# Shorter expert choice on VectorE, the bias added in eight pieces, rows of maxima moved behind a weighing, and the multiply by the reciprocal sums on GpSimd

## The reference

```python
def layer(x):                                    # x: (16, 128, 32, 32) f32
    xs = reshape(ln_c(x), (16, 1024, 128))       # LayerNorm over channels, then 1024 tokens
    q, k, v = 8 heads of 16 each                 # xs @ Wq, Wk, Wv
    att = softmax(q @ k.T / sqrt(16))            # per image and head: 1024 x 1024
    out = (att @ v) @ Wproj + bproj
    x1  = x + reshape(out)
    t   = to_tokens(x1)                          # (16, 1024, 128)
    raw_gates = softmax(ln_t(t) @ w_gating)      # 16 experts
    gate_1, index_1 = max(raw_gates), argmax(raw_gates)
    mask_1 = one_hot(index_1)
    gate_2, index_2 = max, argmax of raw_gates * (1 - mask_1)
    mask_2 = one_hot(index_2)
    gate_1, gate_2 = each / (gate_1 + gate_2 + 1e-9)
    # position of each token in its expert's queue: running counts of mask_1 and mask_2, cut at 256
    # experts: relu(rows @ w1[e]) @ w2[e], weighted by gate_1 and gate_2 and summed per token
    return from_tokens(t + experts(ln_t(t)))
```

## Time and profile before

| what | value |
|---|---|
| three runs | 2253.78, 2254.86, 2256.43 us |
| the profiled execution's own time | 2254.34 us |
| its span in the trace | 2252.5 us |
| TensorE busy | 2106.4 us, 94% |
| VectorE busy | 1841.2 us, 82% |
| ScalarE busy | 1528.6 us, 68% |
| GpSimd busy | 1048.7 us, 47% |
| weight loads on TensorE | 1175.1 us, 52% |

### The profile page before, as it was taken

One profiled execution on the slowest core, in us unless ns is written; L12 is line 12 of the kernel. 1 busy time (PEld: TensorE's weight loads), 2 busy tenths in 40 slices (PEclk: granted clock), 3 DMA queues, 4 the chain that ended last, 5 costly groups with the idle time before them and its releaser, 6 DMA issues. The chain is left out here.

```text
span 2252.5 us, 53329 instructions
## 1 busy us (share of the span) xinstructions
PE 2106.4 (94%) x16914; PEld 1175.1 (52%) x16914; DVE 1841.2 (82%) x4370; ACT 1528.6 (68%) x3169; POOL 1048.7 (47%) x1650
## 2 busy tenths in 40 slices
PE   5999999999999999999999999999969999899996
PEld 2333333334333333334333333333339999899996
DVE  6899999999999999999999999999925445345664
ACT  1777777777777777777777777777646566466552
POOL 3204454454445455454445455444246577455542
PEclk7999999999999999999999999999989999999997
DMA  5223323132323323232323323223162223222586
GB/s 127 48 44 63 60 58 76 36 71 45 69 53 72 61 53 74 37 70 51 67 52 68 71 43 74 39 60 57 40 190 70 71 71 86 78 71 71 159 253 178
DMA packets 135695, 171.09 MB, mean 76 GB/s; under 512 B 31568, under 2 KB 101592, under 8 KB 135414
## 3 DMA queue, kind: packets, MB, share of 16 engines
q1 hardware_dynamic: 118582, 134.25, 27.9%
q0 software_dynamic: 16896, 34.12, 4.3%
HBM read 64.86 MB, written 48.87 MB: 50 GB/s over the span
## 5 line engine op out<-in xcount | busy, mean ns | idle before, releaser
L1009 DVE TENSOR_REDUCE sb_m_red<-banks 128x1 f32<-128x512 f32 x2048 | 1318.8, 678 | 85.6 <-PE banks L1531 79.7
L848 ACT ACTIVATE sb_arena_a<-banks 128x512 f32<-128x512 f32 x2048 | 1088.7, 600 | 329.4 <-PE banks L1555 325.7
L1555 PE MATMUL banks<-sb_arena_b 64*128 64x512 f32 x2048 | 788.7, 460 | 21.5 <-DVE sb_res L1068 9.6
L1531 PE MATMUL banks<-sb_arena_b 62*128 62x512 f32 x2048 | 741.9, 448 | 40.4 <-DVE sb_m_red L1009 27.4
L1531 PEld LDWEIGHTS banks<-sb_arena_b 62*128 62x128 f32 x2048 | 340.7, 188 | 571.7 <-DVE sb_m_red L1009 468.5
L1572 PE MATMUL banks<-sb_arena_a,sb_arena_d 128*32 128x512 f32 x4096 | 546.0, 605 | 11.0 <-DVE sb_o_t L1041 9.3
L777 POOL DMA_INDIRECT sorted_rows<-sb_rows,sb_place x256 | 250.8, 980 | 343.3 <-PE banks L1555 325.4
L1555 PEld LDWEIGHTS banks<-sb_arena_b 64*128 64x128 f32 x2048 | 331.6, 185 | 139.5 <-ACT sb_arena_a L848 95.5
L821 POOL DMA_INDIRECT expert_out<-sb_arena_d x272 | 271.6, 999 | 242.6 <-DVE sb_arena_d L1401 178.1
L1685 PE MATMUL banks<-sb_arena_d,sb_arena_c 128*128 128x128 f32 x2176 | 290.4, 277 | 1.2 <-ACT sb_arena_d L954 0.7
L1694 PE MATMUL banks<-sb_arena_c 128*128 128x128 f32 x2176 | 289.0, 276 | 0.0
(11 more groups left out here) (167 smaller groups left out, 1597.4 us busy)
## 6 DMA issues: line engine op xcount, KB each, us to landing
sb_arena_b<-sb_arena_c SPq DMA_DIRECT2D x768, 64.0 KB, 2.3
sb_arena_d<-sorted_rows SPq DMA_DIRECT2D x272, 66.0 KB
sb_x_in<-in_x_dram SPq DMA_DIRECT2D x16, 512.0 KB, 3.9
sb_res<-in_x_dram SPq DMA_DIRECT2D x16, 512.0 KB, 3.6
...
expert_out<-sb_arena_d POOLq DMA_INDIRECT x272
sorted_rows<-sb_rows,sb_place POOLq DMA_INDIRECT x256
...
```

Source lines behind the costliest of these rows:

```text
L848: nc.scalar.activation(probs[:, u % PRING, :], front("score", b, u), ACT.Exp, scale=SCALE).then_inc(exp_done, 1)
L1009: nc.vector.tensor_reduce(out=m_red[:, s % 2, at:at + 1], in_=ps_max[:, m % MRING, :], axis=AX.X, op=ALU.max).then_inc(max_taken, 1)
L1531: nc.tensor.matmul(ps_max[:, m % MRING, :], qs[rows_of, g, l, half * HALF + t * P:half * HALF + (t + 1) * P], ks[rows_of, g, l, kh * HALF: ...
L1555: nc.tensor.matmul(to, ks[rows_of, g, l, i * P:(i + 1) * P], qs[rows_of, g, l, half * HALF:(half + 1) * HALF], start=True, stop=True).then ...
```

## The change

1. **Expert choice.** The first choice is made on the shifted logits (their maximum is zero), the gates are never normalised before the choice, and ties are resolved by `scalar_tensor_tensor` with two operations in one instruction. VectorE keeps 12 instructions in a stream of its own: `top_logit` at unit 46, `choose_experts` from unit 54 (ten steps), `reciprocal_of_gates` at unit 76. GpSimd takes over scaling and shifting the logits (L708, L713 in the new kernel), one multiply of the second choice (`rank_second`, L718), and eight small instructions that finish the masks and the sum of the two gates (`finish_masks`, L724 to L744).
2. **Division.** `divide` on VectorE keeps transpose and reciprocal (units 4, 5); the multiply by the reciprocal sums is `scale_o` on GpSimd, in its queue; the transpose for the projection moves from unit 7 to 10. `divide` of the next stage waits for it (`o_scaled`).
3. **Bias** in eight instructions of 128 x 128 instead of one of 128 x 1024.
4. **Places on TensorE.** x transposes from units 1 and 5 to 3 and 11, counts from 77 to 78, rows of maxima from slot 24 to slot 26 of each stage. Slot 26 stands right behind a weighing.

The core of the diff (the tables and the new functions; where the new steps are called; the removed steps of `choose_experts` are cut):

```diff
-MSLOT = 24
+MSLOT = 26
-NORMS = 14
+NORMS = 10
...
-XT_AT, QK_AT, V_AT = (1, 5), (33, 41, 44, 48), (62, 66)
-OUT_AT, TOK_AT, LOGITS_AT, COUNT_AT, ROWS_AT = (14, 18), (20, 22), 36, 77, (74, 82)
-GATE_AT, CHOOSE_AT = 38, 44
+XT_AT, QK_AT, V_AT = (3, 11), (33, 41, 44, 48), (62, 66)
+OUT_AT, TOK_AT, LOGITS_AT, COUNT_AT, ROWS_AT = (14, 18), (20, 22), 36, 78, (74, 82)
+TOP_AT, FIRST_AT, GATE_EXP_AT, RECIP_AT = 46, 54, 50, 76
+DIVIDE_AT = (4, 5, 10)
...
+            def scale_o(b, s):
+
+                g, half = s // 2, s % 2
+                wait_apart(gp, gp_passed, norm_steps, norms_before(b, s) + 2)
+                nc.gpsimd.tensor_tensor(out=o_n[:, half, :, D * g:D * (g + 1)], in0=o_t[:, :, 0:D],
+                                        in1=o_rec[:, :].unsqueeze(2).to_broadcast([P, HALF // 32, D]),
+                                        op=ALU.mult).then_inc(o_scaled, 1)
+
             def add_bias(b):
                 wait_apart(gp, gp_passed, res_loaded, 16 * (b + 1))
-                r3 = res[:, :].rearrange("p (j c) -> p j c", j=TB)
-                nc.gpsimd.tensor_tensor(out=r3, in0=r3, in1=bias[:, :].unsqueeze(1).to_broadcast([P, TB, C]),
-                                        op=ALU.add).then_inc(res_ready, 1)
+                for j in range(TB):
+                    nc.gpsimd.tensor_tensor(out=res[:, j * C:(j + 1) * C], in0=res[:, j * C:(j + 1) * C], in1=bias[:, :],
+                                            op=ALU.add).then_inc(res_ready, 1)
...
                 place_v(b, 1)
+                if not first:
+                    scale_o(b - 1, 3)
...
+                for i in range(4):
+                    if not last:
+                        split_qk(b + 1, i)
+                    if not first and i < 2:
+                        (scale_logits, shift_logits)[i](b - 1)
+                    if i == 0:
+                        scale_o(b, 0)
+                if not first:
+                    rank_second(b - 1)
+                    finish_masks(b - 1)
                 if not last:
-                    for i in range(4):
-                        split_qk(b + 1, i)
                     place_v(b + 1, 0)
+                scale_o(b, 1)
                 add_bias(b)
+                if first:
+                    scale_o(b, 2)
                 if not first:
                     for _ in place_rows(b - 1):
                         pass
                     if b == EARLY:
                         keep_counts()
                     for n in range(16 if last else 8):
+                        if n == 2:
+                            scale_o(b, 2)
                         scatter(b - 1, n, at + 96 + (2 if last else 4) * n)
...
+            scale_o(B - 1, 3)
...
-                    if 4 <= u % UNITS < 8 and not (first and u < UNITS):
-                        divide(b, u // UNITS - 1, u % UNITS - 4)
+                    if u % UNITS in DIVIDE_AT and not (first and u < UNITS):
+                        divide(b, u // UNITS - 1, DIVIDE_AT.index(u % UNITS))
...
-                        if u == GATE_AT:
-                            gate = choose(b - 1)
-                        if GATE_AT <= u < GATE_AT + 3:
-                            next(gate)
-                        if u == CHOOSE_AT:
+                        if u == TOP_AT:
+                            top_logit(b - 1)
+                        if u == FIRST_AT:
                             choice = choose_experts(b - 1)
-                        if u >= CHOOSE_AT and u % UNITS not in BUSY:
+                        if FIRST_AT <= u < FIRST_AT + 20 and u % UNITS not in BUSY:
                             next(choice, None)
+                        if u == RECIP_AT:
+                            reciprocal_of_gates(b - 1)
```

More of the change, by code:

```diff
@@ L1040, in divide @@
                     wait(dve, pv_done, 8 * (k + 1))
+                    wait(dve, o_scaled, k)
                     nc.vector.transpose(o_t[:, :, :].rearrange("p n d -> p (n d)"), ps_pv[:, :]).then_inc(norm_steps, 1)
@@ L1112, in choose_experts @@
+                step(nc.vector.tensor_tensor(out=m1, in0=tmp2[:, :, :], in1=wide(small[:, 5, :]), op=ALU.is_equal))
+                yield
                 wait(dve, gate_exp, b + 1)
@@ L1371, in _ @@
             batch(B - 1, False, True)
-            for step in range(4):
+            for step in range(3):
                 divide(B, -1, step)
```

182 lines of the change are left out of this document (95 added, 87 removed).

## The result

The changed kernel takes 2238.59 us (median of four, 2237.93 to 2240.41) against 2254.94 of the kernel before: a ratio of 0.9925, with an interval of 0.9913 to 0.9937. That is 16.4 us less, where 31.9 less were forecast. The direction was right and the time lies in the range, but near its upper end: half of the gain did not come.

A forecast was written before the change was run, and what follows sets the result against it. TensorE and ScalarE were taken to set the pace, with VectorE felt in a few groups. Terms of 1.85 us per image gave 25.9 for images 1 to 14, plus 0.5 and 5.1: 31.5 less, 2223 us, range 2208 to 2240.

The forecast's parts named there:

- What bounds the kernel: Free pace set by TensorE and ScalarE, 2.64 us a group; VectorE felt at three or four places, about 2.5 of 100.8.
- the rival of VectorE as the bound: Every microsecond removed from VectorE would count, 5.3 us per image, giving 2171 us; chance 0.04.
- Expert choice, 0.70 at 51 to 55: Units 51 to 55: a load waited 1.19 for a maximum; moving choice steps off VectorE gains 0.70 us per image.
- 0.49 at 107 to 111: Units 107 to 111, 0.49 us over the free pace: loss taken as gone, since no choice step stands there now.
- Counts, 0.20: Units 75 to 79: 0.51 of waiting for VectorE goes, 0.3 given back at unit 78; gain 0.20 us per image.
- x transposes, 0.59: Unit 1's group gains 0.59 us per image; unit 3 costs what 5 did, unit 11 hides in unit 17's residual wait.
- Multiply, 0.17: Multiply moved to GpSimd: VectorE reaches the residual ahead of unit 17 earlier, gaining 0.17 us per image.
- Rows of maxima, +0.10 - 0.40: Slot 24 to 26, per image: transposes behind the weighing gain 0.10 us, rows late at units 0 and 96 lose 0.40.
- Image 15, 5.1: Image 15 gains 5.1 us once: 2.59 from the stop, 1.11 from the half clock, 1.4 from blocked groups.
- Image 0, 0.5: Image 0, which has no choice, gains 0.5 us.
- The rival of rows that land late (2261): Rows at stage starts take 3.65 us from issue to score everywhere, not 2.68; slower, 2261 us; chance 0.08.
- The rival of GpSimd giving nothing back: Multiply waits in GpSimd's queue or VectorE stands locked out, some 5 us per image; 2252 us; chance 0.06.

## Why the prediction was right and where it failed

The forecast had 1.85 us per image, measured were 0.87. Term by term, with what the runs showed:

- **What bounds the kernel** was right: the free pace is TensorE's and ScalarE's, and VectorE is felt only in a few groups. 18 more instructions of 7.0 us per image cost 0.8, so the rival of VectorE as the bound (2171) falls.
- **Expert choice, 0.70 at 51 to 55**: right, 0.70, and by the cause named: 2.64 in image 0 of the kernel before, which has no choice, and 3.14 again with work put back at 44 to 49.
- **0.49 at 107 to 111**: right in size and wrong in its cause. The text gave it to the choice, with "none at 107" as what is new. There was none at 107 before either: that a step stood behind nearly every maximum "until its end", as the part on the change has it, holds only to unit 77. The last step of the choice in image 8 of the kernel before (VectorE's timeline) ran some 21 us ahead of that group:

```profile
925.41 0.19 DVE L1172 RECIPROCAL sb_small<-sb_small 128x8 f32<-128x8 f32 x1
```

It was the division, by the kernel with the old division, by the kernel before with the transpose at 10, and by the 3.14 of image 0. The size came out right by luck, because the same change moved both.
- **Counts, 0.20**: nothing. The step that failed is "of which I take 0.51 as lost": a load that waits 0.56 for VectorE was followed by one that waited for ScalarE, and that second wait ended at the same time with or without the first, 1.29 after the group's start. The 0.3 given back for the place at 78 was nothing too.
- **x transposes, 0.59**: 0.25 by the groups of units 1 and 3, 0.31 by the run that puts them back (beside rows at slot 26). The gain of 0.54 to 0.59 at unit 1 and the hidden cost at unit 11 were right; "should cost what that did", of unit 3 against unit 5, was not, by 0.29.
- **Multiply, 0.17**: too small. 0.19 shows at units 11 to 15, but off VectorE it is worth 0.60 per image (100.47 with it on VectorE, against 99.87): 0.34 before the residual and 0.24 at 111 to 115, where the transpose alone would have put a new block. The whole division is worth 0.8 to 0.9 per image, more than the choice, and the prediction had 0.17 for it and the 0.49 in the wrong place. GpSimd's longer queue cost nothing in images 0 to 14: 621 ns each, and no wait for it appears. In image 15 the last two transposes for the projection wait 2.3 and 8.0 us for it; the stretch after the last score is 0.4 us longer in all, and whether that is the reason was not tried.
- **Rows of maxima, +0.10 - 0.40**: -0.78 measured. The lateness was predicted well: 0.62 at units 0 and 96 against 0.63, and from issue to score 2.66 (855.21 - 852.55, below) against 2.68. What was wrong is what follows from it. The lateness costs nothing: the group that ends at unit 3 takes 2.64 with it, and so does the one that ends at 99 once the stack DMAs go ahead. But the two DMAs, two units later, hold three stack DMAs in SyncE's queue for which TensorE waits at unit 99 (0.54). The prediction counted the moved step's own DMAs and not what is queued behind them. Behind a weighing the rows cost 3.17 and not less than 3.13.

```profile
852.55 1.36 SPq L423 DMA_DIRECT2D sb_arena_b<-sb_m_row  x2
...
855.21 0.19 PEld L1591 LDWEIGHTS banks<-sb_arena_b 64*128 64x128 f32 x2 [0.44 <-DMA sb_arena_b<-sb_m_row]
```

- **Image 15, 5.1**: 5.0, in part by luck. The stop and the half clock gave 2.57 and 1.11, as forecast (2.59 and 1.11), though in the changed kernel the moved choice alone ends the stop and the pieces add nothing. The other 1.4 was put down to "the groups that are blocked as in other images", and these were not blocked in image 15 (units 51 to 55 took 2.65 and 107 to 111 took 2.60 before). In their place came 0.64 by which the image's first score starts later, 0.49 at 11 to 15, 0.54 at 31 to 35 and 0.27 at 67 to 71, less 0.38 at 39 to 43.
- **Image 0, 0.5**: -1.0. Unit 99 costs 0.54, the score of unit 128 comes 0.64 later (which image 1 gives back), and the rows and unit 32 cost 0.4; units 107 to 111 give 0.49, and x at unit 11 costs nothing in the end (0.56 at 11 to 15, 0.55 given back by unit 23). Unit 1 gives 0.74, but units 3 to 8 take 0.62 more: they lie where the clock is still low after the start (it rises at 65.8 us before and at 66.9 after), and with other kernels they took 4.24 to 5.87. So this part says little of the change.
- **The rival of rows that land late (2261)** did not come: 2.66 at units 0 and 96. It had named the right step and the wrong mechanism. **The rival of GpSimd giving nothing back** falls with 8.3 us lost when the multiply returns to VectorE, though VectorE's own two-input instructions are still stretched beside GpSimd (0.74 against 0.28).

The misses by groups are 0.48 for the rows, 0.34 for x (0.05 at unit 1, 0.29 at unit 3), 0.20 for the counts, and -0.04 at units 11 to 19 (0.21 against 0.17): 0.98, which is 1.85 - 0.87. The prediction as a whole was right in sign and range and twice too large, half of that for one queue, and two of its terms (0.49 per image, and 1.4 of image 15) have the right size for a wrong reason.

## What to carry to other kernels

A wait in front of an instruction is worth its length only if nothing else would have held the next one: look at the instruction after it, and at the same group in an image or loop where the waited-for engine has nothing to do, as image 0 is here for the choice. When a step with DMAs moves, list what stands behind it in the issuing queue and who needs that first. And before a block is put down to some work, find when that work ended: 21 us lay between the choice's last step and the group it was blamed for.

## What the runs showed of the chip

- A VectorE instruction with two SBUF inputs of 128 x 128 took 0.28 us as the median of the 252 additions, 0.44 beside GpSimd instructions of 0.43, 0.74 beside one of 1.28 and 2.25 beside one of 2.35 us. Of these additions, 27 took over 0.5 us, and each of them ended 0.15 us after a GpSimd instruction had ended; so did the one of 2.25 (1602.64 against 1602.49). Maxima, with their input in PSUM, took 0.62 to 0.69 us all through the changed kernel. The Trainium skill ("SBUF — State Buffer", SBUF: two separate sides) has the port pair of the two engines as a lock that is held for the whole instruction; the lengths and ends here agree with it.
- TensorE's clock fell to the lower level (1.2 GHz) for some 3 us in image 15 in five of the traces read here, at unit 45 or 47 after a stop of 2.6 us, or at unit 71 after a wait of 1.03 us for VectorE's transpose; in others with the same wait of 1.03 it stayed at 2.4 GHz. A fall at unit 71 lengthens units 71 to 75 from 4.1 to 5.6 us. It fell in the steady part too: at unit 103 of image 10 in three kernels (x at 1 and 5, the old division, the 18 additions), where units 103 to 107 took 5.2 instead of 3.7, and at unit 18 of image 8 in the kernel before with the transpose at 10. Such a fall in one image is 0.1 in a mean over 14, as large as some of the differences above. What decides was not tried, and why images 8 and 10 were hit is open. The stretch of image 10 with the additions (columns as above):

```profile
1144.90:1148.30 3.40, 3.38 (x14) 1.03 (x14) 2.52 (x6) 1.29 (x4) 1.63 (x2) 0.51 0.07 25
```

- Taking away one stop laid bare others: in the kernel before with the bias in pieces, 2.9 us won at units 43 to 51 came back as 1.1 of waits for VectorE and 1.5 of half clock in the next 25 units.
